# Second attention of a four-stage layer kernel: scores computed twice, once for the row maxima and once already transposed, with the position bias added by TensorE

## The chip, the cores and the metric

One core of one Trainium2 chip runs the whole program in one launch. The metric is device time in microseconds (us), the median of several executions. Smaller is better. One execution, taken by the hardware profiler, gives the rows shown here.

## The reference, cut to what matters

The input is 16 sequences of 512 tokens of width 128. Four layers follow each other, each with a residual and a layer norm: a first attention (cumulative sums), a first mixture of 8 experts, a second attention (softmax with a position bias), a second mixture of 8 experts. The change is in the second attention, and it borrows time in the first expert layer.

```python
table = jax.vmap(_fir_fft, in_axes=(0, None))(coeffs, proto).T
rel = jnp.abs(r[None, :] - r[:, None]).astype(jnp.float32) / max(S - 1, 1)
idx = jnp.clip(jnp.round(rel * (RES - 1)).astype(jnp.int32), 0, RES - 1)
pos_bias = jnp.einsum('ijf,hf->hij', table[idx], Wpos)
q, k, v = jnp.split(jnp.einsum('bsd,ed->bse', x, Wqkv), 3, axis=-1)      # 16 heads of 8 columns
logits = jnp.einsum('bihd,bjhd->bhij', q, k) * scale + pos_bias[None]
attn = jax.nn.softmax(logits, axis=-1)
out = jnp.einsum('bhij,bjhd->bihd', attn, v).reshape(B, S, D)
return jnp.einsum('bsd,ed->bse', out, Wout)
```

The bias of a head depends on the distance of query and key alone, so one line of numbers per head holds it all.

## The kernel before

The program is a chain of five stages with a barrier between each two: `attention_one`, `experts` with tag b, `attention_two` (tiles named c_), `experts` with tag d, `finish`. Each engine has a program of its own, and they meet through semaphores; the order on every engine is written out by hand.

`attention_two` (L1081) goes over 16 sequences, one `body` each. A body is 64 units: 16 heads times 4 blocks of 128 queries, each unit being 128 queries by 512 keys. For one unit:

- TensorE (PE) computes the scores (`scores`, L1351). Queries and keys are split into three bf16 parts and stacked, so the contraction has 72 rows and one bf16 matmul of 512 columns does it. It reads from the stacks `qst` and `kst`, which exist twice, one pair for each of two sequences.
- VectorE (DVE) adds the bias tile from SBUF and takes the row minimum of the negated scores (`biased`, L1613). Its result is a 128x512 tile `sums` and a column `low`.
- ScalarE (ACT) takes the exponential in place (`exps`, L1501).
- PE turns the tile with four f32 transposes (`turn`, L1360).
- ACT copies six of eight turned tiles to SBUF, DVE the other two, units 4 and 5 of each eight (`copy`, L1203; `DVE_TILES`, L1113).
- PE multiplies with the values (`values`, L1373). This is done in 32-column tiles of the array, four heads side by side, once for every second unit. A column of ones in the values gives the softmax's denominator.

PE runs six units ahead with scores and DVE five ahead with the bias; four PSUM banks hold scores. Between the units stand the small jobs of a sequence, called `others` on each engine (L1433, L1542, L1671): the front of the next sequence (`front_turn`, `front_qk`, `front_v`: sum of the expert result, layer norm, projection to q, k, v), the turning and division of a group of four heads (`out_turn`, `out_norm`), the tail of the last sequence (`tail_turn`, `tail_out`, layer norm) and its routing to the experts (`route_turn`, `route_logits`, `route_count`). A small job on PE waits in line for what ACT or DVE must deliver.

SyncE's queue carries, per sequence: `clear_rows` (2 MB of zeros, L171), the parts to DRAM (L1238), six transfers that build the stacks (`stack`, L1249), the load of `x1` (L1231) and the store of `x3` (L1254). GpSimd (POOL) does the power of -1/2 (`power`, L1299), the split in bf16 parts (`split`, L1174 and L1177), the gather and the scatter of rows.

The loop over sequences (`bodies`, L1210) has the first and the last body written out and seven passes of a hardware loop over two bodies each.

`experts` (L842) with tag b goes over 24 blocks of 512 tokens. Its SyncE queue loads `x` and `w` for each block (L921, L922), four buffers deep, and GpSimd has nothing to do there after one memset (L935).

## Time and profile before

| | us |
|---|---|
| median of 3 runs | 2395.94 |
| lowest, highest | 2393.09, 2398.47 |
| the profiled execution | 2393.4 |
| its span, first to last instruction | 2391.6 |

Busy time over the span: PE 2020.0 us (84%), weight loads 1300.1 us (54%, beside PE), DVE 1641.1 us (69%), ACT 1533.0 us (64%), POOL 797.4 us (33%). The granted TensorE clock is 0.939 of full speed over the span.

A share of the whole span mixes five stages with different limits. The second attention is a little over half of the span, so it has to be read by itself, in a window of its own. In the rows below a group is named by line, engine, operation and tiles; "out<-in" are the program's names.

### The profile page before, as it was taken

The page shows a single profiled execution, that of the slowest core. Times are in us where ns is not written, and L with a number is a line of the kernel's source. Part 1 is how long each engine was busy: PE and PEld are TensorE (multiplying, and loading weights), DVE is VectorE, ACT ScalarE, POOL GpSimd, SP SyncE. Part 2 cuts the span into 40 slices and gives each one's busy share as a digit, 9 for nine tenths or more (in the row PEclk, how much of TensorE's full clock was granted, in tenths as well). Part 3 has the DMA queues.
Part 4 walks back from the last instruction along what each step waited for, and adds up shares of the span by engine and source line. Part 5 has one row for each costly group of instructions (what it writes and reads, how often), then busy time and mean ns, then how long its engine had stood idle before and what let it go on. Part 6 is the DMA issues. An engine that isn't in the chain of part 4 may idle for free. (4 is left out here: it accounts for less than half of the span.)

```text
span 2391.6 us, 49680 instructions
## 1 busy us (share of the span) xinstructions
PE 2020.0 (84%) x14348; PEld 1300.1 (54%) x14348; DVE 1641.1 (69%) x4785; ACT 1533.0 (64%) x3427; POOL 797.4 (33%) x804
## 2 busy tenths in 40 slices
PE   8478887887494799999999999999999999779886
PEld 6256555566372455555555555555555555446553
DVE  6377888887212678877877788787778787633276
ACT  3355655564141688888888888888888888523221
POOL 4467888887101211222122122212211220000176
PEclk9788999999696899999999999999999999889998
DMA  3451332321263303320332033213311330034332
GB/s 112 149 211 67 106 105 103 103 101 62 96 214 126 112 31 97 107 87 34 97 107 81 28 107 107 57 53 108 102 44 70 107 93 11 10 130 164 112 103 83
DMA packets 114183, 227.10 MB, mean 95 GB/s; under 512 B 11684, under 2 KB 39332, under 8 KB 111604
## 3 DMA queue, kind: packets, MB, share of 16 engines
q1 hardware_dynamic: 105748, 207.36, 26.3%
q0 software_dynamic: 8192, 16.79, 2.2%
q8 instruction: 116, 1.90, 0.3%
q14 instruction: 127, 1.04, 0.1%
HBM read 177.86 MB, written 121.23 MB: 125 GB/s over the span
## 5 line engine op out<-in xcount | busy, mean ns | idle before, releaser
L1613 DVE CUSTOM_DVE_ANT_0 c_sums<-c_s,bias 128x512 f32<-128x512 f32 x1024 | 673.6, 687 | 180.2 <-PE c_s L1351 140.7
L1501 ACT ACTIVATE c_sums<-c_sums,c_low 128x512 f32<-128x512 f32 x1024 | 735.3, 743 | 39.1 <-DVE c_low L1613 28.2
L1360 PE MATMUL c_turned<-ident,c_sums 128*128 128x128 f32 x4096 | 633.4, 277 | 29.8 <-ACT c_pT L1203 27.8
L1360 PEld LDWEIGHTS c_turned<-ident,c_sums 128*128 128x128 f32 x4096 | 497.4, 142 | 181.2 <-ACT c_pT L1203 91.0
L1203 ACT COPY c_pT<-c_turned 128x512 f32<-128x512 f32 x768 | 454.7, 592 | 129.2 <-PE c_turned L1360 128.5
L1351 PE MATMUL c_s<-c_kst,c_qst 72*128 72x512 bf16 x1024 | 399.0, 391 | 45.9 <-DMA c_qst<-parts_d 27.5
L1373 PE MATMUL c_o<-c_pT,c_vst 128*32 128x256 f32 x4096 | 328.2, 393 | 0.7 <-ACT c_pT L1203 0.7
L1299 POOL TENSOR_TENSOR c_rstd<-c_ve,minus_half 128x4 f32<-128x4 f32 x32 | 32.9, 1027 | 638.1 <-DVE c_ve L122 638.1
L1203 DVE COPY c_pT<-c_turned 128x512 f32<-128x512 f32 x256 | 176.6, 690 | 86.0 <-PE c_turned L1360 83.9
L1351 PEld LDWEIGHTS c_s<-c_kst,c_qst 72*128 72x128 bf16 x1024 | 102.3, 100 | 232.3 <-issue 123.8
L520 ACT ACTIVATE v<-a_bank,gain 128x64 f32<-128x64 f32 x768 | 165.7, 344 | 53.9 <-DVE vp L734 53.9
L386 PE MATMUL a_bank<-wv,xT 128*128 128x512 f32 x256 | 153.4, 685 | 19.6 <-ACT v L520 15.1
L528 ACT COPY oT<-a_bank 128x512 f32<-128x512 f32 x128 | 69.5, 586 | 148.5 <-PE a_bank L407 148.5
L587 POOL TENSOR_TENSOR q<-q,vp 128x1024 f32<-128x1024 f32 x48 | 124.9, 2602 | 104.4 <-DVE vp L734 104.0
L598 POOL TENSOR_TENSOR s<-q,v 128x1024 f32<-128x1024 f32 x48 | 142.9, 2978 | 0.1
L1306 POOL DMA_INDIRECT zs_d<-c_xs,c_slot x64 | 62.7, 980 | 218.6 <-DVE c_slot L1669 202.0
L734 DVE TENSOR_TENSOR vp<-a_bank,ez 128x512 f32<-128x512 f32 x96 | 64.8, 687 | 102.4 <-PE a_bank L386 100.4
L415 PEld LDWEIGHTS a_bank<-wo,oT 128*128 128x128 f32 x1024 | 127.3, 200 | 14.3 <-issue 14.3
L415 PE MATMUL a_bank<-wo,oT 128*128 128x128 f32 x1024 | 129.6, 282 | 0.0
L1373 PEld LDWEIGHTS c_o<-c_pT,c_vst 128*32 128x32 f32 x4096 | 81.4, 108 | 87.3 <-issue 85.8
L407 PE MATMUL a_bank<-ident,o 128*128 128x128 f32 x512 | 80.4, 308 | 51.6 <-DVE o L750 50.8
L750 DVE TENSOR_TENSOR o<-o,r 128x1024 f32<-128x1024 f32 x64 | 123.6, 1951 | 0.0
(248 smaller groups left out, 2795.4 us busy)
## 6 DMA issues: line engine op xcount, KB each, us to landing
xs_d<-in_zeros SPq DMA_DIRECT2D x16, 2048.0 KB
zs_d<-in_zeros SPq DMA_DIRECT2D x16, 2048.0 KB, 24.8
c_kst<-parts_d SPq DMA_DIRECT2D x48, 384.0 KB
c_qst<-parts_d SPq DMA_DIRECT2D x48, 384.0 KB
parts_d<-c_parts SPq DMA_DIRECT2D x32, 384.0 KB, 2.5
d_w<-in_wd SPq DMA_DIRECT2D x24, 384.0 KB, 3.2
b_w<-in_wb SPq DMA_DIRECT2D x24, 321.0 KB, 3.1
bias_d<-line_d SPq DMA_DIRECT2D x16, 448.0 KB
```

Source lines behind the costliest of these rows:

```text
L386: nc.tensor.matmul(v_ps[h][:], xT[s.par][:, t, :], wv[:, 512 * h:512 * h + 512], start=True, stop=True).then_inc(sem("v_ready"), 1)
L415: mm = nc.tensor.matmul(y_ps[:, t * W:(t + 1) * W], oT[t % 2][:, k, :], wo[:, k, :], start=(k == 0), stop=(k == HA // P - 1))
L520: ins = nc.scalar.activation(dst[:, h * A:(h + 1) * A], v_ps[half][:, k * A:(k + 1) * A], ACT.Copy, scale=gain[s.par][:, t, h:h + 1])
L587: nc.gpsimd.tensor_tensor(q[:, t, :], q[:, t - 1, :], vp[t % 2][:], ALU.add).then_inc(sem("q_ready"), 1)
L598: nc.gpsimd.tensor_tensor(s1[s.par][:, t, :], q[:, t - 1, :], v2[t % 2][:], ALU.add).then_inc(sem("s1_ready"), 1)
L750: v.tensor_tensor(heads(o[t % 2][:]), heads(o[t % 2][:]), r[s.par][:, t, :].unsqueeze(2).to_broadcast([P, H, A]), ALU.mult).then_inc(sem(" ...
L1203: engine(pT[r % 2][:, :, m // 2, m % 2 * P:(m % 2 + 1) * P], pT_ps[m % 2][:]).then_inc(sem(copied(s, n)[0]), 1)
L1351: nc.tensor.matmul(s_ps[n % BANKS][:], qst[s.par][:, h, t * P:(t + 1) * P], kst[s.par][:, h, :], start=True, stop=True).then_inc(sem("s_ps ...
L1360: mm = nc.tensor.transpose(pT_ps[n % 2][:, c, :], sums[n % BUFS][:, c * P:(c + 1) * P], keep.ident[:])
L1373: mm = nc.tensor.matmul(o_ps[ARRAY * i:ARRAY * (i + 1), r % 2 * 2 * P:(r % 2 + 1) * 2 * P], vst[s.par][:, c, f:f + ARRAY], pT[r % 2][:, c, ...
L1501: nc.scalar.activation(sums[b][:], sums[b][:], ACT.Exp, bias=low[b][:], scale=-1.0).then_inc(sem("exp_done"), 1)
L1613: v.tensor_tensor_reduce(sums[n % BUFS][:], s_ps[n % BANKS][:], bias, 1.0, 3.0e38, ALU.add, ALU.min, low[n % BUFS][:]).then_inc(sem("low_r ...
```

## The change

The second attention is computed in two passes over the scores.

- **Pass one** (`scores`, `tops`): as before, but in group order, with DVE taking the row maximum and throwing the sum away. It runs 16 slots, half a sequence, ahead of pass two. A slot is two units.
- **The maxima** of a group of four heads (16 columns) are turned by PE (`tops_turn`), written as two bf16 parts (`tops_high` on ACT, `tops_low` on DVE), sent to DRAM and from there into rows 126 and 127 of `qst` (SyncE's `tops`). The same rows of `kst` hold -1. Rows 72 to 125 are zeros.
- **Pass two** (`below`, `biased`): a matmul over all 128 rows gives the scores transposed and less the maximum. Four bf16 matmuls in 32-column tiles add the bias from a tile `line`, in which each of 96 partitions holds the bias line shifted by one element, in three bf16 parts. ACT takes the exponential from PSUM straight into the layout that `values` needs. The four f32 transposes and the copies of ACT and DVE are gone, and so is the sum tile in SBUF as an input of ACT.
- `values` runs once per slot, right behind `biased`.
- One pair of stacks instead of two; the stacks are built in four parts, one for each group of four heads.
- The small jobs are divided over more slots, and the front is made two sequences ahead instead of one.
- `line` is prepared on GpSimd in `experts` b: three bf16 parts to DRAM, then 16 transfers that spread it, each let go by one finished block.
- At the start DVE clears partitions 64 to 127 of both stacks with two memsets of 8192 bf16 elements per partition. Three bodies are written out before the loop and three behind it; the loop has five passes of two.

```diff
+        def spread_line(pool):
+            pool.wait_ge(sem("line_out"), 16)
+            LAST = LINE - ARRAY
+            flat = keep.line[:].rearrange("r h d n -> r (h d n)")
+            PIECES = 4
+            for k in range(PIECES):
+                first, past = LINE // PIECES * k, min(LINE // PIECES * (k + 1), LAST)
+                for a in range(LINE_PARTS + 1):
+                    pool.wait_ge(sem("y_ps"), PIECES * k + a + 1)
+                    src = bass.AP(io["lparts_d"].tensor, a % LINE_PARTS * LINE + first, [[1, ARRAY], [1, past - first]])
+                    pool.dma_start(flat[ARRAY * a:ARRAY * (a + 1), first:past], src).then_inc(sem("line_in"), 16)
...
-    LEAD = 6
-    DVE_LEAD = 5
-    ACT_LEAD = 2
-    BANKS = 4
-    BUFS = 8
-    DVE_TILES = (4, 5)
+    SLOTS = ALL // 2
+    PER = TILES // 2
+    LEAD = 2 * PER
+    BANKS = 3
...
         def bodies(eng, body, own=None, per=0):
-            body(at(0), tail=False)
-            with eng.Fori(0, NB // 2 - 1) as i:
+            for k in range(3):
+                body(at(k), Flags(k > 0, True, True))
+            with eng.Fori(0, (NB - 6) // 2) as i:
...
+                def stack(s, j):
+                    for w in range(2):
+                        sp.wait_ge(sem(f"parts_out{w}"), 16 * s.b + 16)
+                        apart(sp, sem("sp_passed"))
+                    need(sp, sem("u_ps"), ALL * (s.b - 1) + TILES * (j + 1))
...
+                def tops(s, j):
+                    sp.wait_ge(sem("m_ready"), group_of(s, j) + 1)
+                    sp.dma_start(io["tops_d"].rearrange("a i p -> i a p"), mT[:]).then_inc(sem("m_out"), 16)
+                    sp.wait_ge(sem("m_out"), 16 * group_of(s, j) + 16)
+                    apart(sp, sem("sp_passed"))
+                    sp.dma_start(qst[ROWS_MAX:P, G * j:G * j + G, :].rearrange("r h n -> r (h n)"),
+                                 io["tops_d"].rearrange("a i p -> a (i p)")).then_inc(sem(f"m_in{j}"), 16)
...
+                def body(s, on):
+                    if not isinstance(s.b, int) or s.b > 0:
+                        stack(s, 3)
+                    if on.front:
+                        load(s.ahead().ahead())
+                    tops(s, 1)
+                    if on.nxt:
+                        put_parts(s.ahead())
+                        stack(s.ahead(), 0)
+                    tops(s, 2)
+                    if on.tail:
+                        store(s.back())
+                    if on.nxt:
+                        stack(s.ahead(), 1)
+                    tops(s, 3)
                     clear_rows(sp, "zs_d", s.b, io, sem("rows_clear"))
+                    if on.nxt:
+                        stack(s.ahead(), 2)
+                        tops(s.ahead(), 0)
...
+                def below(s, n):
+                    j, c, i = unit(n)
+                    if n % TILES == 0:
+                        pe.wait_ge(sem(f"m_in{j}"), 16 * s.b + 16)
+                    need(pe, sem("exp_done"), freed(s, n))
+                    h = G * j + i
+                    nc.tensor.matmul(u_ps[bank_of(n)][:], kst[:, h, c * P:(c + 1) * P], qst[:, h, :],
+                                     start=True, stop=False, skip_group_check=True)
+                def biased(s, n):
+                    j, c, i = unit(n)
+                    for k in range(P // ARRAY):
+                        u = P - ARRAY - ARRAY * k
+                        mm = nc.tensor.matmul(u_ps[bank_of(n)][ARRAY * k:ARRAY * (k + 1), :].rearrange("k (t q) -> k t q", t=T), pick[:],
+                                              line[:, G * j + i, T - 1 - c:DELTA - c, u:u + P], start=False, stop=True,
+                                              skip_group_check=True)
+                    mm.then_inc(sem("u_ps"), 1)
...
+                def body(s, on):
+                    for p in range(SLOTS):
+                        u = 2 * (p + LEAD)
+                        if u < ALL:
+                            scores(s, u)
+                            scores(s, u + 1)
+                        elif on.nxt:
+                            scores(s.ahead(), u - ALL)
+                            scores(s.ahead(), u - ALL + 1)
+                        below(s, 2 * p)
+                        below(s, 2 * p + 1)
+                        biased(s, 2 * p)
+                        biased(s, 2 * p + 1)
+                        if p >= 2:
+                            values(s, (p - 2) // 2, p % 2)
+                        elif on.tail:
+                            values(s.back(), SETS - 1, p)
+                        others(s, p, on)
...
                 def exps(s, n):
-                    act.wait_ge(sem("low_ready"), ALL * s.b + n + 1)
-                    b = n % BUFS
-                    nc.scalar.activation(sums[b][:], sums[b][:], ACT.Exp, bias=low[b][:], scale=-1.0).then_inc(sem("exp_done"), 1)
+                    act.wait_ge(sem("u_ps"), ALL * s.b + n + 1)
+                    if n % G == 0:
+                        need(act, sem("pv_done"), SETS * s.b + n // G - 1)
+                    nc.scalar.activation(pT[n // G % 2][:, n % G, :], u_ps[bank_of(n)][:], ACT.Exp).then_inc(sem("exp_done"), 1)
...
+                def body(s, on):
+                    for p in range(SLOTS):
+                        exps(s, 2 * p)
+                        others(s, p, on)
+                        exps(s, 2 * p + 1)
+                        if p % PER == 1 and (p > 1 or on.tail):
+                            out_copy(*((s, p // PER - 1) if p > 1 else (s.back(), GROUPS - 1)))
...
                 v = nc.vector
                 own = Own(dve, sem("own"), sem("dve_passed"))
+                v.memset(minus[:], -1.0).then_inc(sem("minus_ready"), 1)
+                v.memset(kst[64:P], 0.0).then_inc(sem("pad_ready"), 1)
+                v.memset(qst[64:P], 0.0).then_inc(sem("pad_ready"), 1)
```

On PE the small jobs stand at the end of a slot: `tail_out` in slot 9, `route_logits` in slot 17, `front_qk` in slots 30 and 31, each a slot or two behind the turn that feeds it. ACT's copy for them stands between the two exponentials of slots 9, 17, 30 and 31.

## Rows read from the trace of the kernel before

**Rows 1.** Page, section 2: 40 slices of the span, PE's busy tenths and its clock

```profile
PE   8478887887494799999999999999999999779886
PEclk9788999999696899999999999999999999889998
```

**Rows 2.** Stretches: length; busy PE, PEld, DVE, ACT, POOL; clock; DMA share; GB/s

```profile
739.00:789.50 50.50, 7.28 (x16) 3.53 (x17) 8.69 (x24) 2.55 (x7) 10.50 (x13) 0.50 0.40 127
789.50:2072.70 1283.20, 1203.73 (x10128) 729.20 (x10128) 1017.89 (x3346) 1099.82 (x2006) 251.48 (x280) 0.99 0.24 75
650.00:700.00 50.00, 49.85 (x305) 36.98 (x305) 8.30 (x12) 23.73 (x39) 0.00 (x0) 1.00 0.66 215
```

**Rows 3.** PE in order of time in the regular part: start us, length us

```profile
1267.69 0.64 PE L1373 MATMUL c_o<-c_pT,c_vst 128*32 128x256 f32 x8
1268.26 0.39 PE L1351 MATMUL c_s<-c_kst,c_qst 72*128 72x512 bf16 x1
1268.49 0.60 PE L1360 MATMUL c_turned<-ident,c_sums 128*128 128x128 f32 x4
1268.93 0.38 PE L1351 MATMUL c_s<-c_kst,c_qst 72*128 72x512 bf16 x1
...
1271.96 0.66 PE L1360 MATMUL c_turned<-ident,c_sums 128*128 128x128 f32 x4 [0.22 <-ACT c_pT L1203]
```

**Rows 4.** The last products with the values, PE in order of time

```profile
2070.07 1.94 PE L1373 MATMUL c_o<-c_pT,c_vst 128*32 128x256 f32 x32 [0.73 <-ACT c_pT L1203]
```

**Rows 5.** Small jobs on PE in one sequence, in order of time

```profile
1286.92 1.13 PE L1394 MATMUL c_misc<-c_xT,c_wq 128*128 128x512 f32 x2
1287.88 0.38 PE L1351 MATMUL c_s<-c_kst,c_qst 72*128 72x512 bf16 x1
...
1295.79 0.66 PE L1406 MATMUL c_misc<-ident,c_att 128*128 128x128 f32 x4
1296.28 0.38 PE L1351 MATMUL c_s<-c_kst,c_qst 72*128 72x512 bf16 x1
```

**Rows 6.** Groups by line: busy us, mean ns of one

```profile
L1862 ACT ACTIVATE e_gate<-e_bank 128x512 f32<-128x512 f32 x32 | 19.1, 597 | 84.7 <-PE e_bank L1821 84.7
L1631 DVE COPY c_x<-c_x 128x512 f32<-128x512 f32 x16 | 6.8, 423 | 0.0
```

**Rows 7.** DVE in order of time: two bias additions that follow each other

```profile
790.90 0.69 DVE L1613 CUSTOM_DVE_ANT_0 c_sums<-c_s,bias 128x512 f32<-128x512 f32 x1
791.51 0.69 DVE L1613 CUSTOM_DVE_ANT_0 c_sums<-c_s,bias 128x512 f32<-128x512 f32 x1
```

**Rows 8.** A back edge of the loop: a stretch, and PE's first row after it

```profile
1350.00:1354.00 4.00, 2.85 (x13) 2.16 (x14) 2.64 (x7) 2.46 (x5) 0.00 (x0) 0.74 0.04 8
1351.15 0.39 PE L1351 MATMUL c_s<-c_kst,c_qst 72*128 72x512 bf16 x1 [2.70 <-issue]
```

**Rows 9.** Start of the second attention, all engines in order of time

```profile
745.05 1.28 POOL L1326 MEMSET c_vst<- 128x668 f32 x2
746.75 0.69 DVE L1593 TENSOR_TENSOR c_yb<-c_yb,prob 128x512 f32<-128x512 f32 x1 [7.45 <-DMA c_yb<-ys_d,c_rows]
...
766.28 2.30 SPq L1249 DMA_DIRECT2D c_qst<-parts_d  x3
...
789.50 3.37 PE L1351 MATMUL c_s<-c_kst,c_qst 72*128 72x512 bf16 x7 [27.52 <-DMA c_qst<-parts_d]
```

**Rows 10.** Page, section 6: transfers, KB each, median us to landing

```profile
zs_d<-in_zeros SPq DMA_DIRECT2D x16, 2048.0 KB, 24.8
...
parts_d<-c_parts SPq DMA_DIRECT2D x32, 384.0 KB, 2.5
...
b_x<-xs_d SPq DMA_DIRECT2D x24, 256.0 KB, 2.6
...
c_x<-x_d SPq DMA_DIRECT2D x16, 256.0 KB, 22.6
```

More of the change, by code:

```diff
@@ L1198, in copy, with unit @@
[L1198 to L1208 removed]
+        def unit(n):
+            j, n = n // TILES, n % TILES
+            return j, n // G, n % G
@@ L1556, in others @@
+                    if on.tail and p == 21:
                         route_exp(s.back())
-                def body(s, tail=True, front=True):
-                    for j in range(GROUPS):
-                        for n in range(SLOTS):
-                            k = SLOTS * j + n
-                            if later(s, k + ACT_LEAD, front):
-                                exps(*later(s, k + ACT_LEAD))
-                            if n % ROUND_SLOTS not in DVE_TILES:
-                                copy(s, k, act, nc.scalar.copy)
-                            others(s, j, n, tail, front)
+                    if on.nxt and p == 27:
+                        tops_high(s.ahead(), 0)
@@ L1605, in biased, with stats @@
[L1605 to L1614 removed]
+                def stats(src, st, some):
+                    for t in some:
+                        own.did(v.bn_stats(st[:, t, :], src[:, t, :]))
@@ new lines, in spread, with scaled @@
+                def spread(st, mv, ve, ready):
+                    own.wait(alone=True)
+                    for t in range(T):
+                        own.did(v.bn_aggr(mv[:, t, :], st[:, t, :]))
+                    own.wait()
+                    v.tensor_scalar(ve[:], mv[:, :, 1], EPS, None, ALU.add).then_inc(ready, 1)
+                def scaled(src, dst, mv, rstd, some):
+                    for t in some:
+                        ins = v.tensor_scalar(dst[:, t, :], src[:, t, :], mv[:, t, 0:1], rstd[:, t:t + 1], ALU.subtract, ALU.mult)
+                    return ins
@@ L1694, in body @@
-                def body(s, tail=True, front=True):
-                    for j in range(GROUPS):
-                        for n in range(SLOTS):
-                            k = SLOTS * j + n
-                            if later(s, k + DVE_LEAD, front):
-                                biased(*later(s, k + DVE_LEAD))
-                            if n % ROUND_SLOTS in DVE_TILES:
-                                copy(s, k, dve, v.tensor_copy)
-                            others(s, j, n, tail, front)
@@ L1704, in _, with early @@
-                front_sum(at(0))
-                front_stats(at(0))
-                front_apply(at(0), 1)
-                split(at(0), dve, v, own)
-                for n in range(DVE_LEAD):
-                    biased(at(0), n)
+                def early(s, p, on):
+                    if on.tail and p == 10:
+                        tail_sum(s.back())
+                    if on.tail and p == 18:
+                        route_tops(s.back())
+                    if p == 29:
+                        out_norm(s, 2)
@@ L1934, in program @@
         stage(attention_one)
+        keep.line = sb("spread_line", [P, H, DELTA, UPAD], BF16)
         if stages >= 2:
```

600 lines of the change are left out of this document (387 added, 213 removed).

## Prediction, before the result was known

> **What bounds the kernel now.** First the page's 40 slices, to see the stages: PE is at nine tenths from slice 15 to 34 with the clock near full, and that stretch is the second attention [rows 1]. Then the busy time by stretch, to leave the other stages out: the loop of the second attention lasts 1283.2 us, 80.2 for each of 16 sequences; PE is busy for 1203.7 of them, ACT for 1099.8, DVE for 1017.9 [rows 2]. So PE is the fullest engine, and the change is worth what it takes out of PE's line, its pauses included. That is read in PE's own order of time, from start to start, since matmuls overlap. A score matmul holds PE 0.22 to 0.23 us, four transposes 0.44, a step of `values` 0.57 (1267.69 to 1268.26) [rows 3].
>
> **PE per slot of two units, before.** Two scores 0.44, two turns 0.88, one step of `values`. The last 32 instructions of `values`, with nothing between, take 1.94 us for four steps, less some 0.2 for the end of the last: 0.43 a step [rows 4]. Against 0.57 that leaves 0.14 for going back from 32-column tiles to the whole array [rows 3]. Going in costs about 0.10 (estimate: a turn holds PE 0.53 when `values` follows it, 0.44 when not). Sum 0.44 + 0.88 + 0.43 + 0.24 = 1.99.
>
> **PE per slot, after.** Two scores 0.44. Two `below`, bf16 of 512 columns like a score, 0.44. Eight matmuls of `biased`, in two sets of four side by side: no row shows bf16 in such tiles. The nearest is `values`: 8 f32 matmuls of 256 columns in 0.43, so four of them side by side take 0.213; f32 runs at half the rate per column (two of 512 columns hold PE 0.96 [rows 5], one bf16 0.22), so a set of bf16 with 512 columns moves the same bytes and should also take 0.213. The bounds are that, and no overlap at all, 4 x 0.213 = 0.85. I take 0.215 a set, 0.43 for both, since the f32 row has the full overlap and the same bytes. `values` 0.43, one way in and out 0.24, as before. Sum 1.98. **The two forms cost PE the same**: a transpose set of 0.44 is exchanged for 0.22 + 0.215. What the change can win is only PE's pauses.
>
> **The floor of a sequence.** 32 slots x 1.98 = 63.4. Small jobs: seven turns of four transposes at 0.49 = 3.4 (1295.79 to 1296.28 is one of them); the projection of q 0.96 (1286.92 to 1287.88) [rows 5]; k, v, output and logits stream as much or less, I take 0.9 each, and 0.5 for the counts: 4.1. That is 8.5. New are four `tops_turn`, one transpose each, some 0.15 = 0.6 (a quarter of 0.44 and a little). Sum 9.1, floor 63.4 + 9.1 = 72.5 against 80.2 now, so 7.7 us per sequence are pauses today: PE waits for a copy of ACT or DVE from the two turned banks (0.22 at 1271.96 [rows 3]), and at each of six back edges of the loop nothing comes for 2.70 us and the clock is at 0.74 of full for the next four [rows 8], together some 4.7.
>
> **What takes their place.** The chain sum, exponential, turn, copy is gone. ACT has 64 exponentials straight from PSUM; the nearest row without a bias operand is a Silu of that shape, 597 ns [rows 6], so 38 us and some 7 of copies in 72. DVE has 64 x 0.61 = 39 us of maxima [rows 7] and about 16.6 us of small work, as now: 56 of 72, with work of at most 2.6 us in the fullest slots against 2.0 and three PSUM banks to even it out. Neither is a bound. But four small jobs get a new wait. Output, logits and both projections on PE stand at the end of a slot (1.98), and ACT's copy for them stands behind the first exponential of the same slot. That starts when `biased` of the first unit is done, 0.88 + 0.10 + 0.215 and 0.17 of latency, at 1.4; the exponential holds ACT 0.5, the copy 0.6: ready at 2.5, **0.6 us late, four times: 2.4 us per sequence**. Behind the waiting matmul all of PE stands, scores of the next slot included. ACT and DVE then wait for those. I add 1 us per sequence for other coincidences. Four back edges instead of six: 4 x 4.7 = 19.
>
> **Sum of the loop.** 16 x 72.5 = 1160. The first sequence has no tail (-3.7), the last two no front (-5.7), and the last 16 slots have no scores (-7): 1143.5. Waits 2.4 x 15 and 1 x 16: 52. Back edges 19. Together 1214.5, and 1.7 for the last products.
>
> **The start.** Now the first score starts at 789.50, since the stacks, issued until 768.6, land only then, and the first gathered rows reach DVE at 746.75 [rows 9]. After: two memsets on DVE stand ahead of that. No DVE memset is in the trace. POOL clears 2 x 668 elements in 1.28, which gives 7.8 us for 8192 and 15.7 for both; DVE's fastest copy, 512 elements in 423 ns [rows 6], gives 6.8 each by length. I take 15.7: from 739.3 to 755, so 8.5 late (if they run twice as fast, 7.5 us of idle time hides nearly all). The Trainium skill ("VectorE: DVE Perf Modes", section "Zero memsets can be issued as uint32 (trn2)") says that a memset takes one cycle per element whatever the type, and half of that for bf16 zeros issued as uint32; that would be either end of the same bounds. The first quarter of the stacks should land 6 us after its issue instead of 21 to 24, so scores start at about 784. Then 32 units come before the first `below`, at DVE's pace: 0.61 x 32 = 20 us, to 804, and the maxima's way through DRAM ends about then. The loop ends at 804 + 1216 = 2020, against 2072 now: -52.
>
> **Experts b.** The 16 transfers of `line` are some 0.46 MB each, about one per block of 3.9 us, beside 215 GB/s and a DMA share of 0.66 while PE is full [rows 2]: 118 GB/s more, and 215 / 0.66 = 326 in all is just what there is. A block's input lands in 2.6 us today [rows 10] and is due after one block; later landing stops PE. Bounds 0 and 25 us; I take 6. The split on GpSimd is hidden by the plan of the blocks. The rest is unchanged. **Total -46**: 2393.4 - 46 = 2347 in the profiled execution, whose time is 2.5 under the median: 2350.
>
> **Rivals.** **A, slower: the maxima come late.** Each group's maxima must be in `qst` four to five slots after DVE has them, 9 to 11 us; two transfers that follow each other cost 5 (2.5 each, as the parts [rows 10]). They stand in SyncE's line behind a quarter of the stacks and behind 2 MB of zeros. Before, 256 KB of `x1` behind the stacks took 22.6 us and the zeros 24.8 [rows 10]: small transfers do wait for big ones. A quarter is 6 us, the zeros alone some 6 (2 MB at the 326 GB/s above); I find 5 us of slack for the next sequence's first group. If quarters take twice as long, it is used up; 5 us beyond that cost 15 x 5 = 75: 2350 + 75 = 2425. For: the 22.6. Against: zeros are issued some 14 us earlier. **B, slower: four bf16 streams don't fit side by side.** A quarter more per set, 0.054 x 1024 = 55: 2405; no overlap of pairs, 0.215 x 1024 = 220: 2570. For: no row of bf16. Against: the f32 row. The Trainium skill ("TensorE: Matmul & The Clock Gate", section "Measured speedup vs the span model") measured a speedup of 2.38 for three column tiles, not 3, about the first of these prices; the trace's four f32 streams come close to 4. **C, faster: the waits vanish**, since ACT runs further ahead than I think, memsets and experts cost nothing: 52 + 8.5 + 6 less, 2285. **D: nothing comes of it**: DVE's lumps stop the scores for 3 us per sequence: 2350 + 46 = 2396.
>
> **How the numbers follow.** My forecast (2315 to 2385) 0.50; A 0.19; B 0.08; C 0.13; D 0.10. 0.2% is 4.8 us, what a measurement of this kernel can tell from none. D is spread over both sides of it, as are the weak forms of A. Faster 0.70, same 0.05, slower 0.25. The range leaves out the better half of C and B's and A's upper parts: 2300 to 2440.
>
> **What would show it.** Right: PE's order of time in a slot has 0.22, 0.22, 0.22, 0.22, then 16 instructions of 32-column tiles in about 0.9, slots of 2.0 without a small job, 2.6 plus the job in slots 9, 17, 30 and 31 with PE waiting for ACT's copy, and about 76 us per sequence. DVE busy for three quarters, ACT for under two thirds. Wrong: PE waiting for a transfer into `qst` (A), more than 0.25 us per set of `biased` (B), scores waiting for DVE (D), PE's experts b blocks longer than 3.9 us by over 1.

## The result, and the profile after the change

The changed kernel takes **2328.02 us** (median of 4 runs, 2325.22 to 2330.99), beside 2396.62 us for the kernel before (4 runs, 2393.09 to 2398.47): a ratio of 0.972, 95% interval 0.970 to 0.973, or 68.6 us less. Forecast were 2350 us and a range of 2300 to 2440. The profiled execution has a span of 2325.9 us, 65.7 less than before.

The page of the changed kernel: busy times, the 40 slices, and the costliest groups with busy us, mean ns of one, and the idle time ahead of them.

```profile
PE 1985.4 (85%) x15436; PEld 1034.3 (44%) x15436; DVE 1502.4 (65%) x4596; ACT 1078.8 (46%) x2723; POOL 807.6 (35%) x827
PE   8488787877388499999999999999999999679886
PEclk9689999999699699999999999999999999889998
L1622 ACT ACTIVATE c_pT<-c_u 128x512 f32<-128x512 f32 x1024 | 574.6, 596 | 552.1 <-PE c_u L1429 552.1
L1777 DVE CUSTOM_DVE_ANT_0 c_sums<-c_s,bias 128x512 f32<-128x512 f32 x1024 | 665.1, 687 | 254.2 <-PE c_s L1411 229.5
```

PE is again at nine tenths, from slice 15 to 34 as before [rows 1], but of a shorter span. ACT fell from 1533.0 us to 1078.8, DVE from 1641.1 to 1502.4, and both stand idle mostly because PE has not delivered. So PE sets the pace as before. By stage, in the two profiled executions; an expert stage begins with its first GpSimd memset, the second attention with DVE's first instruction (739.1 and 765.7 us):

| stage | before | after | difference | forecast |
|---|---|---|---|---|
| up to experts b | 626.6 | 628.8 | +2.2 | 0 |
| experts b | 112.5 | 136.9 | +24.4 | +6 |
| second attention | 1361.6 | 1272.5 | -89.1 | -52 |
| experts d and finish | 290.9 | 287.7 | -3.2 | 0 |
| span | 2391.6 | 2325.9 | -65.7 | -46 |

The sum is 20 us off, out of two errors of opposite sign: experts b lost 18 more, and the second attention won 37 more. That the sum is nearer than its terms is luck.

**The regular part**, PE in order of time (start, length), one slot from `scores` to `scores`:

```profile
1223.70 0.60 PE L1411 MATMUL c_s<-c_kst,c_qst 126*128 126x512 bf16 x2
1224.14 0.60 PE L1421 MATMUL c_u<-c_qst,c_kst 128*128 128x512 bf16 x2
1224.66 0.61 PE L1429 MATMUL c_u<-spread_line,c_pick 128*32 128x512 bf16 x8
1225.11 0.60 PE L1443 MATMUL c_o<-c_pT,c_vst 128*32 128x256 f32 x8
1225.64 0.60 PE L1411 MATMUL c_s<-c_kst,c_qst 126*128 126x512 bf16 x2
```

Starts lie 0.44, 0.52, 0.45 and 0.53 us apart: 1.94 us a slot, with nothing waited for. The way into the 32-column tiles is the 0.08 over 0.44 behind `below`, the way out the 0.10 over 0.43 behind `values`.

**PE's waits** from 900 to 1900 us (us in all, times, longest), the whole list of the changed kernel:

```profile
PE c_s L1411 <- issue: 11.5, 4, 3.0
PE c_misc L1469 <- ACT c_xT L1638: 7.7, 13, 0.6
PE c_misc L1486 <- ACT c_xT L1657: 7.4, 14, 0.5
PE c_misc L1469 <- ACT c_qk L1643: 7.3, 13, 0.6
PE c_misc L1498 <- ACT c_xT L1661: 6.9, 13, 0.5
PE c_s L1411 <- DVE c_tops L1777: 2.3, 10, 0.2
```

Four times per sequence 0.5 to 0.6 us for a copy of ACT, four back edges of up to 3.0 us, and next to nothing else. No line names a transfer, and none does from 765 to 2030 us: the maxima were never late. The same turn of a small job, one sequence apart, gives the period, 74.26 us:

```profile
1211.30 0.66 PE L1480 MATMUL c_misc<-ident,c_att 128*128 128x128 f32 x4
...
1214.33 1.16 PE L1486 MATMUL c_misc<-c_wout,c_xT 128*128 128x128 f32 x8 [0.53 <-ACT c_xT L1657]
...
1285.56 0.66 PE L1480 MATMUL c_misc<-ident,c_att 128*128 128x128 f32 x4
```

Before, the same turn came after 78.86 us (1216.93 to 1295.79 [rows 5]). These are sequences without a back edge of the loop. The four with one last 78.63 to 79.02 us, so a back edge costs 4.4 to 4.8.

**The start**, DVE and PE in order of time:

```profile
766.83 3.47 DVE L1721 MEMSET c_kst<- 64x4096 uint32 x1 [0.91 <-issue]
771.11 3.47 DVE L1722 MEMSET c_qst<- 64x4096 uint32 x1 [0.80 <-issue]
...
802.48 2.59 PE L1411 MATMUL c_s<-c_kst,c_qst 126*128 126x512 bf16 x5
...
822.98 1.06 PE L1421 MATMUL c_u<-c_qst,c_kst 128*128 128x512 bf16 x2
```

The first score comes 36.8 us after the stage's first instruction (50.4 before [rows 9]), the first `below` 57.3 after it.

**Experts b.** First the ten microseconds from 650 of the changed kernel (length; busy PE, PEld, DVE, ACT, POOL; clock; DMA share; GB/s), then what PE waited for there between 650 and 765:

```profile
650.00:660.00 10.00, 9.14 (x58) 6.54 (x57) 1.38 (x2) 4.37 (x7) 0.99 (x2) 1.00 1.01 268
...
PE b_bank L1093 <- DMA b_x<-xs_d: 15.2, 10, 3.7
```

Before, the stage ran at a share of 0.66 and 215 GB/s with PE never idle [rows 2]. Now the share is at its top while only 268 GB/s move, and PE waits ten times for the input of a block. The waits are not the whole cost. One of them, in order of time, and the stretch 666 to 667 us behind it:

```profile
663.91 0.66 PE L1093 MATMUL b_bank<-ident,b_x 128*128 128x128 f32 x4 [2.37 <-DMA b_x<-xs_d]
...
669.57 0.60 PE L1093 MATMUL b_bank<-ident,b_x 128*128 128x128 f32 x4
...
666.00:667.00 1.00, 1.00 (x7) 1.00 (x6) 0.00 (x0) 0.69 (x1) 0.00 (x0) 0.50 0.98 330
```

Behind each of the three longest waits (2.37, 3.12 and 3.69 us) the granted clock is 0.50, its lower level of 1.2 GHz, and that block takes 5.7 to 6.6 us instead of 3.94. Of the 24.4 us, 15.5 are waits (16.5 us behind the stage's first input against 1.0 before), some 6 are the clock (estimate: busy time times the missing clock, over slices of 1 us), and 1.0 is a later first block; the last 2 are not traced.

### The profile page after: what moved, and what is told of

It is laid out like the page before. It is cut to its first block and busy times, and to the rows that moved or that the text cites. A ratio compares the mean times of both kernels' runs of the same rounds, so it can differ in the third digit from the quotient of the medians.

```text
span 2325.9 us, 49229 instructions
## 1 busy us (share of the span) xinstructions
PE 1985.4 (85%) x15436; PEld 1034.3 (44%) x15436; DVE 1502.4 (65%) x4596; ACT 1078.8 (46%) x2723; POOL 807.6 (35%) x827
## 5 line engine op out<-in xcount | busy, mean ns | idle before, releaser
L1622 ACT ACTIVATE c_pT<-c_u 128x512 f32<-128x512 f32 x1024 | 574.6, 596 | 552.1 <-PE c_u L1429 552.1
L1411 PE MATMUL c_s<-c_kst,c_qst 126*128 126x512 bf16 x1024 | 319.0, 389 | 16.9 <-issue 11.5
L1429 PE MATMUL c_u<-spread_line,c_pick 128*32 128x512 bf16 x4096 | 317.2, 387 | 0.0
L1443 PE MATMUL c_o<-c_pT,c_vst 128*32 128x256 f32 x4096 | 310.9, 381 | 0.6 <-ACT c_pT L1622 0.5
L1421 PE MATMUL c_u<-c_qst,c_kst 128*128 128x512 bf16 x1024 | 307.7, 381 | 0.2 <-ACT c_pT L1622 0.2
L1443 PEld LDWEIGHTS c_o<-c_pT,c_vst 128*32 128x32 f32 x4096 | 123.1, 110 | 107.4 <-ACT c_pT L1622 4.0
L1429 PEld LDWEIGHTS c_u<-spread_line,c_pick 128*32 128x32 bf16 x4096 | 61.8, 94 | 217.7 <-issue 217.7
L1421 PEld LDWEIGHTS c_u<-c_qst,c_kst 128*128 128x128 bf16 x1024 | 100.2, 98 | 121.1 <-issue 5.8
L1411 PEld LDWEIGHTS c_s<-c_kst,c_qst 126*128 126x128 bf16 x1024 | 82.7, 100 | 158.9 <-DVE c_tops L1777 101.9
L737 DVE TENSOR_TENSOR vp<-a_bank,ez 128x512 f32<-128x512 f32 x96 | 64.8, 687 | 106.8 <-PE a_bank L389 105.0
L418 PEld LDWEIGHTS a_bank<-wo,oT 128*128 128x128 f32 x1024 | 126.7, 199 | 14.4 <-issue 14.4
L1356 POOL TENSOR_TENSOR c_rstd<-c_ve,minus_half 128x4 f32<-128x4 f32 x16 | 16.7, 1046 | 298.4 <-DVE c_ve L1746 298.4
```

The source lines that it names most:

```text
L418: mm = nc.tensor.matmul(y_ps[:, t * W:(t + 1) * W], oT[t % 2][:, k, :], wo[:, k, :], start=(k == 0), stop=(k == HA // P - 1))
L1411: nc.tensor.matmul(s_ps[bank_of(n)][:], qst[0:ROWS_MAX, h, t * P:(t + 1) * P], kst[0:ROWS_MAX, h, :], start=True, stop=True).then_inc(sem( ...
L1421: nc.tensor.matmul(u_ps[bank_of(n)][:], kst[:, h, c * P:(c + 1) * P], qst[:, h, :], start=True, stop=False, skip_group_check=True)
L1429: mm = nc.tensor.matmul(u_ps[bank_of(n)][ARRAY * k:ARRAY * (k + 1), :].rearrange("k (t q) -> k t q", t=T), pick[:], line[:, G * j + i, T - ...
L1443: mm = nc.tensor.matmul(o_ps[ARRAY * i:ARRAY * (i + 1), half * 2 * P:(half + 1) * 2 * P], vst[s.par][:, c, f:f + ARRAY], pT[r % 2][:, i, h ...
L1622: nc.scalar.activation(pT[n // G % 2][:, n % G, :], u_ps[bank_of(n)][:], ACT.Exp).then_inc(sem("exp_done"), 1)
```

## The experiments

The twelve kernels ran in three groups on three chips. The kernel before took 2400.5 us beside the first group, 2496.1 beside the second and 2488.0 beside the third, so times are compared inside a group or as ratios to the kernel before. Only the third group has the changed kernel itself; the first is set beside the result, where the kernel before took 2396.6, and the 2331 of the 72 rows bears that out. Stage lengths are read between the same two instructions in each trace: "experts b" from its first GpSimd memset to DVE's memset of `kst` (138.0 in the changed kernel), "second attention" from there to the first GpSimd memset of experts d (1271.4). Among the kernels that leave the transfers as they are, experts b ranges from 132.4 to 138.0, so a few us there mean nothing.

| kernel | chip | us | ratio to before | experts b | second attention |
|---|---|---|---|---|---|
| no transfers | 1 | 2301.79 (1 run) | | 114.3 | 1272.3 |
| copy first | 1 | 2284.69 | 0.952 (0.949-0.954) | 136.1 | 1230.4 |
| one stream | 1 | 2330.41 (1 run) | | 133.5 | 1270.4 |
| 72 rows | 1 | 2331.18 | 0.971 (0.969-0.973) | 136.0 | 1273.4 |
| two edges | 2 | 2370.23 | 0.950 (0.947-0.953) | 133.3 | 1294.9 |
| 24 transfers | 2 | 2370.30 | 0.948 (0.945-0.951) | 126.2 | 1308.3 |
| bias twice | 2 | 2579.46 (1 run) | | 132.4 | 1509.5 |
| three together | 2 | 2320.84 | 0.929 (0.927-0.932) | 131.5 | 1250.8 |
| changed kernel | 3 | 2369.34 | 0.953 (0.950-0.956) | 136.5 | 1311.0 |
| split clearing | 3 | 2360.95 | 0.949 (0.946-0.951) | 120.0 | 1317.1 |
| three, split | 3 | 2301.76 | 0.926 (0.924-0.928) | 122.1 | 1254.9 |
| two edges again | 3 | 2363.11 | 0.950 (0.948-0.952) | 133.9 | 1296.6 |

**Are the transfers the cause of the longer experts b?** All 16 transfers of `spread_line` are left out and one GpSimd memset clears the line, so the output lacks the bias.

```diff
-            for k in range(PIECES):
-                first, past = LINE // PIECES * k, min(LINE // PIECES * (k + 1), LAST)
-                for a in range(LINE_PARTS + 1):
...
-                    pool.dma_start(flat[ARRAY * a:ARRAY * (a + 1), first:past], src).then_inc(sem("line_in"), 16)
...
+            nc.gpsimd.memset(keep.line[:], 0.0).then_inc(sem("line_in"), 16)
...
```

> Left out: the 16 transfers that spread the bias line in experts b; GpSimd clears the tile instead, so the output is computed without the bias. Theory (the transfers and the blocks' own loads share the 16 DMA engines, and loads that land late stop PE): experts b falls back from 136.9 us to about 113 us, blocks every 3.94 us from first to last, the landing of b_x back from 3.9 to 2.6 us, the total 2328 - 23 = 2305. Rival (GpSimd's split of the line, its semaphore waits or the plan cost the time, not the transfers): experts b stays above 125 us, since the split is still there. The second attention does not change under either.

Experts b shrinks from 138.0 to 114.3 us while the second attention stays (1272.3), and the time is 2301.8. The same ten microseconds as above in this kernel:

```profile
650.00:660.00 10.00, 10.00 (x64) 7.50 (x63) 1.38 (x2) 5.42 (x9) 4.66 (x1) 1.00 0.55 176
```

Share 0.55 and PE full. The split of the line is still there, so the transfers are what lengthens the stage: 24 us.

**Are the four waits worth what they seem?** ACT's copies of the slots where PE waits stand ahead of the slot's first exponential.

```diff
                     for p in range(SLOTS):
+                        if p in (9, 17, 30, 31):
+                            others(s, p, on)
                         exps(s, 2 * p)
-                        others(s, p, on)
+                        if p not in (9, 17, 30, 31):
+                            others(s, p, on)
                         exps(s, 2 * p + 1)
```

> ACT's copy for the small jobs stands ahead of the first exponential in slots 9, 17, 30 and 31, instead of behind it; nothing else is changed. Theory (PE is the only bound of the loop and loses 0.53 to 0.61 us four times per sequence to this order): the four waits of PE go to about 0, a sequence goes from 74.3 to 72.1 us, the total falls by 2.2 x 15 = 33 us to 2295 (2290 to 2302). Rival 1 (the exponential that is now late by 0.5 us stops PE instead, at below of the next slot or at values): total within 10 us of 2328, with new waits of PE for ACT's exponential. Rival 2 (DVE's maxima are as near to the bound as PE): gain under 15 us, with PE waiting for DVE's maxima.

2284.69 us, 43 under the result and 5 below the range expected; the second attention is 41.0 us shorter. All of PE's waits that are left between 900 and 1900 us, and the same place as above, in order of time:

```profile
PE c_s L1411 <- issue: 8.8, 4, 2.3
PE c_s L1411 <- DVE c_tops L1780: 2.3, 10, 0.2
...
1197.82 0.66 PE L1480 MATMUL c_misc<-ident,c_att 128*128 128x128 f32 x4
...
1200.25 1.16 PE L1486 MATMUL c_misc<-c_wout,c_xT 128*128 128x128 f32 x8
1201.25 0.60 PE L1411 MATMUL c_s<-c_kst,c_qst 126*128 126x512 bf16 x2
...
1202.21 0.62 PE L1429 MATMUL c_u<-spread_line,c_pick 128*32 128x512 bf16 x8
```

The projection follows its turn after 2.43 us instead of 3.03. Nothing is given back: `biased` follows `scores` after 0.96 us in both kernels (1201.25 to 1202.21 here), so the exponential that is late by one copy stops nothing. The period falls from 74.26 to 71.77 us (1197.82 to 1269.59), 15 x 2.49 = 37 us, and the four back edges cost 2.7 less: 40 of the 41.

**Do four bf16 streams lie side by side?** Three of the four matmuls of each `biased` are left out, so the bias reaches a quarter of the rows only.

```diff
-                    for k in range(P // ARRAY):
+                    for k in range(1):
                         u = P - ARRAY - ARRAY * k
```

> Left out: three of the four column tiles of the bias matmuls (12 of 16 are gone per pair of units), so the bias is missing for three quarters of the keys. Theory (four bf16 streams of 512 columns run side by side in the time of one): PE's step from the start of the bias matmuls to values stays at 0.44 us for two units, the slot at 1.94, the total within 6 us of 2328. Rival (the streams share a port and are only partly side by side, one set costing more than one stream): the step falls below 0.44 towards its share; were they serial in pairs, it would be 0.22 per stream now and the time would fall by 0.2 per slot, some 100 us. A single stream of 512 bf16 columns for each of two units can't take less than 0.43 in all if it is the same tile.

2330.41 us, and the second attention lasts 1270.4 us against 1271.4. The slot in this kernel, PE in order of time:

```profile
1223.30 0.60 PE L1411 MATMUL c_s<-c_kst,c_qst 126*128 126x512 bf16 x2
1223.74 0.60 PE L1421 MATMUL c_u<-c_qst,c_kst 128*128 128x512 bf16 x2
1224.27 0.39 PE L1429 MATMUL c_u<-spread_line,c_pick 128*32 128x512 bf16 x1
1224.28 0.42 PE L1443 MATMUL c_o<-c_pT,c_vst 128*32 128x256 f32 x3
1224.50 0.38 PE L1429 MATMUL c_u<-spread_line,c_pick 128*32 128x512 bf16 x1
1224.52 0.78 PE L1443 MATMUL c_o<-c_pT,c_vst 128*32 128x256 f32 x5
1225.24 0.60 PE L1411 MATMUL c_s<-c_kst,c_qst 126*128 126x512 bf16 x2
```

One stream takes 0.23 us to the next, four took 0.22: the slot is 1.94 in both. `values` now starts 0.01 us behind the first bias matmul, in the tiles that it leaves free; but the slot is no shorter, since one tile still has both bias matmuls and its part of `values` to do. What that tile does is the price of a set, and the other three streams are free.

**What does a set cost, and is PE really the bound?** Each unit gets a second set of four with a weight tile of zeros.

```diff
+                    for k in range(P // ARRAY):
+                        u = P - ARRAY - ARRAY * k
+                        nc.tensor.matmul(u_ps[bank_of(n)][ARRAY * k:ARRAY * (k + 1), :].rearrange("k (t q) -> k t q", t=T), nil[:],
+                                         line[:, G * j + i, T - 1 - c:DELTA - c, u:u + P], start=False, stop=False,
+                                         skip_group_check=True)
...
```

> Each unit gets four more bf16 matmuls in 32-column tiles, with a weight tile of zeros, ahead of the four that add the bias; nothing is left out and the sums stay the same. Theory: in the second attention PE is what sets the pace, and a set of four side by side costs what the stack of four costs in the forecast, 0.215 us: 1024 sets x 0.215 = 220 us more, 2328 + 220 = 2548. If a set only needs the time of one stream without the way in and out, and the way out of the tiles was 0.10 of it, 1024 x 0.11 = 113: 2441. Rival: ACT or DVE sets the pace in most slots; then the first part of the added time vanishes in their slack and the kernel stays under 2400.

2579.46 us, 209 more than the two other kernels on that chip that keep the order of ACT (2370). PE in order of time:

```profile
1223.27 0.61 PE L1413 MATMUL c_s<-c_kst,c_qst 126*128 126x512 bf16 x2
1223.72 0.60 PE L1423 MATMUL c_u<-c_qst,c_kst 128*128 128x512 bf16 x2
1224.24 0.40 PE L1431 MATMUL c_u<-spread_line,c_nil 128*32 128x512 bf16 x4
1224.47 0.39 PE L1436 MATMUL c_u<-spread_line,c_pick 128*32 128x512 bf16 x4
1224.68 0.39 PE L1431 MATMUL c_u<-spread_line,c_nil 128*32 128x512 bf16 x4
1224.90 0.39 PE L1436 MATMUL c_u<-spread_line,c_pick 128*32 128x512 bf16 x4
1225.12 0.60 PE L1450 MATMUL c_o<-c_pT,c_vst 128*32 128x256 f32 x8
```

A set takes 0.21 to 0.23 us. 1024 x 0.22 = 225; the stage grew by 201 (1509.5 against 1308.3). The rest are waits of PE that the longer slot swallows: those for ACT's four copies fell from 35 us to 24, those for ACT's exponentials from 16.4 to 3.0 and those for DVE's maxima from 15.9 to 1.6, while 13 us came up of which the profile names no releaser. Nine tenths of what is added to PE's line is paid: it is the bound.

**Do the filled rows cost anything?** The scores of pass one read 72 rows instead of 126.

```diff
-                    nc.tensor.matmul(s_ps[bank_of(n)][:], qst[0:ROWS_MAX, h, t * P:(t + 1) * P], kst[0:ROWS_MAX, h, :],
+                    nc.tensor.matmul(s_ps[bank_of(n)][:], qst[0:ROWS_QK, h, t * P:(t + 1) * P], kst[0:ROWS_QK, h, :],
```

> The scores of pass one contract over the 72 rows that hold data instead of 126 (the pad rows are zeros), as before the change; nothing else is changed. Theory (the filled rows cost nothing and bring nothing while PE is kept busy by other work): total within 5 us of 2328, granted clock as before at 0.98 to 1.00 in the loop. Rival (the clock follows how much of the array is in use, so the filled rows keep it up): the clock falls in parts of the loop, and the time rises by 10 us or more.

2331.18 us, ratio 0.971 as the changed kernel; its second attention lasts 1273.4, and the granted clock from 900 to 1900 us is 0.99 in both. The filled rows neither cost nor bring time that can be told from noise.

**Two back edges instead of four.** Five bodies are written out on each side of the loop. The first run had no changed kernel on its chip beside it, so it was run again.

```diff
-            for k in range(3):
+            for k in range(5):
                 body(at(k), Flags(k > 0, True, True))
-            with eng.Fori(0, (NB - 6) // 2) as i:
+            with eng.Fori(0, (NB - 10) // 2) as i:
...
+            body(at(NB - 5), Flags(True, True, True))
+            body(at(NB - 4), Flags(True, True, True))
...
```

> Five sequences are written out ahead of the hardware loop and five behind it, so the loop has three passes and two back edges instead of four; nothing else is changed. Theory: each back edge costs PE 2.7 to 3.0 us in which nothing comes and about 2 us at a lower clock behind it, 4.7 in all, so two fewer give 9.4 us: 2328 - 9 = 2319, ratio to the kernel before 0.968 against 0.972 of the changed kernel, and PE's waits at c_s for nothing that the profile shows fall from 4 times to 2. Rival: the written-out sequences cost as much in another place (more instructions to fetch once each), then 2324 to 2332 and the same ratio as the changed kernel.

> Two back edges instead of four and nothing else, now beside the changed kernel on the same chip. Theory: 9.4 us under it (2 x 4.7), 0.4 percent. Rival: the sequences written out cost as much elsewhere, no difference over 3 us. In the one profile at hand PE's waits at the back edge are 2 instead of 4, 6.3 us instead of 11.9, so that the direct part should be 5.6 us at least.

The first run gave a ratio of 0.950, far below the expected 0.968, which is the chip's doing. On the third chip 2363.11 against 2369.34: 6.2 us, with intervals of the ratios that overlap, so that the time alone does not tell 9.4 from 3. PE's wait at the back edges from 790 to 2030 us, the changed kernel of that chip first:

```profile
PE c_s L1411 <- issue: 12.0, 4, 3.4
```

```profile
PE c_s L1413 <- issue: 6.3, 4, 3.2
```

The direct part of 5.7 us is there. The stage is 14.3 us shorter in these profiles, and 13.4 between the two kernels of the second chip; 3.0 of the 14.3 are waits behind the pauses told of below (7.8 less for ACT's exponentials, 4.8 more for DVE's maxima), and the slower clock behind an edge is in the rest. From turn to turn, as above, the four edges of the changed kernel cost 2.6 to 4.8 us each on this chip, 16.0 together, and the two here 8.3. That is 7.8 for two. But a sequence written out also lasts 75.8 to 76.3 us there and one in the loop 77.5 to 77.7, where the result's trace has 73.9 and 74.3; with four more written out, that is as much again, and why is open. The forecast 9.4 lies between what the times and the traces say, and that two edges alone bring it is not shown.

**What of the transfers costs the time?** They become 24 of half the size, one for each block; the last 32 partitions are cleared by GpSimd. First in one memset ahead of them:

```diff
-            PIECES = 4
+            PIECES = 8
+            nc.gpsimd.memset(keep.line[ARRAY * LINE_PARTS:P], 0.0).then_inc(sem("line_clear"), 1)
...
-                for a in range(LINE_PARTS + 1):
-                    pool.wait_ge(sem("y_ps"), PIECES * k + a + 1)
+                for a in range(LINE_PARTS):
+                    need(pool, sem("y_ps"), LINE_PARTS * k + a)
...
```

> The bias line is spread in 24 transfers of half the size, one for each block of experts b, and its last 32 partitions are cleared by GpSimd in place of four transfers. 5.4 MB are moved instead of 7.2 MB, evenly over the stage. Theory: the 24 us that experts b became longer come from the bandwidth that the 16 large transfers take in single blocks (DMA share 1.0, loads of x late by more than the buffers give); with the load spread, about 120 GB/s less at the peak, the stage lasts 113 to 120 us instead of 137: 2328 - 17 to - 24 = 2304 to 2311, ratio 0.962 to 0.965. Rival: the sum of bytes sets it (then 24 x 5.4 / 7.2 = 18 us remain of the 24): 2322, ratio 0.969. Second rival: the layout of the source rows, each starting one element further, costs by the number of rows and not by their size: then 24 transfers of 32 rows against 16 of 32 are no cheaper, 2328 or more.

The stage still lasted 126.2 us, 7 less than the 133.3 of its neighbour on the chip, and the time, 2370.30, is the neighbour's; the expected 0.962 to 0.965 can't be judged there, without the changed kernel. The experiment had a fault of its own, seen in the GpSimd rows of the kernel with all three edits:

```profile
654.28 23.99 POOL L930 MEMSET spread_line<- 32x28672 bf16 x1 [2.02 <-DMA lparts_d<-b_lparts]
678.22 2.47 POOL L936 DMA_DIRECT2D spread_line<-lparts_d  x5
...
693.14 1.11 PE L1095 MATMUL b_bank<-ident,b_x 128*128 128x128 f32 x4 [7.79 <-DMA b_x<-xs_d]
```

The memset holds GpSimd for 24 us, and five transfers then leave at once, with a sixth in the same 3 us. PE, which had not waited since the second block, stands still for 7.79 us. So the clearing was split into eight memsets, each ahead of three transfers:

```diff
             for k in range(PIECES):
                 first, past = LINE // PIECES * k, min(LINE // PIECES * (k + 1), LAST)
+                nc.gpsimd.memset(flat[ARRAY * LINE_PARTS:P, first:past], 0.0).then_inc(sem("line_clear"), 1)
```

> The changed kernel itself, as the measure for the three others, since the edits of two edges and of 24 transfers ran on a chip where the kernel before took 2496 us instead of 2397 and no run of the changed kernel stands beside them. Expected: if that chip comes again, the two of these runs that share the loop and the waits with it (two edges 2370, 24 transfers 2370) put it at 2375 to 2385, ratio 0.952 to 0.955; on a chip like the first, 2328 to 2333, ratio 0.971.

2369.34 us, ratio 0.953, as expected for a chip of this kind.

> The bias line is again spread in 24 half-size transfers, one for each block of experts b, but the last 32 partitions are cleared by GpSimd in eight memsets of 3 us, one ahead of every third transfer, instead of one of 24 us that held back the first transfers and let four of them go together. Theory: the 24 us of experts b come from transfers that meet in the same block; spread evenly, with 5.4 MB instead of 7.2, the stage falls from 137 us to 113 to 122: 15 to 24 us under the changed kernel of the same job, 0.6 to 1.0 percent. Rival: bytes alone decide, three quarters of them cost 18 us: 6 us under it. Second rival: the number of rows decides, 24 x 32 against 16 x 32: no gain or up to 10 us slower.

Experts b 120.0 us against 136.5 of the changed kernel on that chip: 16.5 less, inside the forecast of this theory, while three quarters of the bytes would have left 18 of 24. The time fell by only 8.4 us, with intervals of the ratios that overlap: in the profiled execution experts b began 8.3 us later (638.9 against 630.6) and the second attention lasted 6.2 longer, neither of which the edit touches. First the 80 us from 660 in the changed kernel on that chip, then in this one:

```profile
660.00:740.00 80.00, 64.77 (x360) 45.22 (x359) 10.38 (x15) 28.67 (x45) 6.40 (x13) 0.96 0.90 243
```

```profile
660.00:740.00 80.00, 76.32 (x453) 54.04 (x452) 13.14 (x19) 35.46 (x56) 28.62 (x26) 1.00 0.88 252
```

Mean share and bandwidth are nearly the same, and PE is busy for 76.3 us instead of 64.8. That is not an equal load: the line now takes half as much per block, 0.23 MB instead of 0.46, and PE gets through more blocks. Two causes are at work, and they are only in part taken apart. The mean load is one: beside the blocks' 215 GB/s the line wanted 118, 333 in all, where 268 to 275 move at a share of one. That stretches 16 blocks of 3.94 us by 13 to 15 us (estimate), about what PE waited; with half the line per block, 274 are wanted and almost nothing is left. Lumps are the other: the two kernels with the single memset move the same bytes as the two with the split one, and have experts b of 126.2 and 131.5 us against 120.0 and 122.1.

**The three together.**

> Three edits together: ACT makes the copy of a small job ahead of the first exponential of the slot where PE waits for it (slots 9, 17, 30 and 31), the loop has two back edges instead of four, and the bias line is spread in 24 even transfers. Theory: they lie in different places, so they add up: 44 us of the first (2328 - 2285, as measured alone), 9 of the second, 17 to 24 of the third: 2251 to 2258, ratio to the kernel before 0.939 to 0.943. Rival: without the waits another limit is near (DVE at 65 percent of the span, ACT's line), and part of it is taken back: 2265 to 2280.

2320.84 us, 49.5 less than its two neighbours on the second chip, each of which has one of the three edits. The ratio 0.929 is below the expected 0.939 to 0.943, but it can't be compared with one from another chip.

> ACT's copy of four small jobs first, two back edges, and the 24 transfers with the split clearing, together. Theory: 44 + 9 + 15 to 24 us under the changed kernel of the same job, ratio to it 0.967 to 0.971, and 0.939 to 0.943 to the kernel before on a chip like the first. Rival: once the waits are gone, pauses of DVE and ACT reach PE, as on the chip where the three together took 2321: then 50 us or less under the changed kernel, ratio to it 0.979 or more.

With the split clearing 2301.76 us, 67.6 less than the changed kernel beside it (ratio 0.9715): experts b 14.4, second attention 56.1. The edits add up, to the lower end of the 68 to 77 that were expected, and the rival of 50 or less did not come, and this version beats both kernels: 0.926 of the kernel before.

**Pauses of ACT and DVE on two of the chips.** The changed kernel itself is 41 us slower on the third chip than in the result, nearly all in the second attention (1311.0 against 1271.4). Its waits from 790 to 2030 us, then an ACT row:

```profile
PE c_u L1421 <- ACT c_pT L1622: 18.2, 15, 1.5
PE c_s L1411 <- DVE c_tops L1777: 17.0, 23, 1.6
...
1112.15 1.08 ACT L1622 ACTIVATE c_pT<-c_u 128x512 f32<-128x512 f32 x2 [3.36 <-remote]
```

ACT stands still for over 3 us, 15 times in 1000 us, and the profile names no instruction of the core as the cause; in the result's trace there is no such wait. ACT's and DVE's slack takes up most of each, and PE sees 1.6 us of one at most: 18.2 + 17.0, less the 5.1 that stand in the same lines in the result, is 30.1 of the 39.6. What the pauses are stays open. On these chips the kernel before lost more (2488 against 2397), so the change is worth 4.7% there and 2.8% in the result; the trace of the kernel before on such a chip was not taken, so why is open too.

## Why the prediction was right, and where its terms were off

The direction and the mechanism were right: PE is the bound, the two forms cost PE much the same, and what the change wins is pauses. A sequence without a back edge fell from 78.86 to 74.26 us. The total was nearer than its terms: with experts b as forecast, the result would have been 2310 us, 40 under the forecast, so part of the small miss is luck.

- **The slot, 1.98 forecast, 1.94 measured.** Scores and `below` 0.44 each and a set of 0.22 were right. The way in and out was taken as 0.24, and is 0.08 + 0.10. 512 slots x 0.04 = 20 us, the largest single part of the 30 us by which the loop was shorter (1186 us from the first `below` at 822.98 to the last `values` at 2009.1, against 1216). The term had been taken from single differences of start times, 0.57 for `values` [rows 3] and 0.53 for a turn ahead of it; it is small, but stands there 512 times.
- **The four waits**, forecast at 0.6 us in slots 9, 17, 30 and 31, were measured at 0.5 to 0.6 there and nowhere else; moving the copies took them away. The prediction's own sum, ready at 2.5 in a slot of 1.98, gives 0.5 and not 0.6. The period is 74.26 us against 75.9, of which 32 x 0.04 = 1.3 is the slot. The 1 us for other coincidences was needed: 62.1 for slots, 9.1 for small jobs and 2.2 for waits leave 0.9.
- **Back edges** 4.7 each: 4.4 to 4.8 were measured, of which 3.0 at most is waiting.
- **The start.** Memsets were taken at 7.8 us each, and take 3.47 for 8192 bf16 elements per partition, as 4096 words. The slower bound was chosen because only an f32 row was there. The other bound, that they run twice as fast and hide, held: DVE's front sum came 1.5 us late, at 9.1 us after the stage's first instruction. The Trainium skill ("VectorE: DVE Perf Modes", section "Zero memsets can be issued as uint32 (trn2)") says that zeros in bf16 can be issued as half as many uint32 words, and the row has that form; that it halves the time no run here shows, since none has the other form at this size. The first `below` came 7.6 us earlier than forecast, of which 7.0 are this term; the 20 us for the first 32 maxima were right (20.5).
- **Experts b, the step that failed.** 6 us were taken between bounds of 0 and 25; it was 24.4. The working added mean rates, 215 + 118 GB/s against 326, and found that it just fits. That 326 was 215 divided by a share of 0.66, as if a share of one were worth as many bytes for every kind of transfer. Measured, a share of 1.01 moved 268 GB/s, and PE waited up to 3.7 us for one block's input. The slower clock behind the longest waits, some 6 us, was in neither bound. Half as much of the line per block, spread over all 24, took 16.5 us of the loss away.
- **Rival A** (maxima late) did not occur: no wait names `qst`, and the transfer behind which they might stand, 2 MB of zeros, lands sooner than before (24.8 us [rows 10]), as the page of the changed kernel shows:

```profile
zs_d<-in_zeros SPq DMA_DIRECT2D x16, 2048.0 KB, 10.0
```

- **Rival B** (streams not side by side) is refuted by the kernel with one stream and priced by the one with two sets. The Trainium skill ("TensorE: Matmul & The Clock Gate", section "Measured speedup vs the span model") gives 2.38 for three column tiles; here four bf16 tiles of 512 columns cost what one costs, so the measurement decides against it for this shape.
- **Rival C** (the waits vanish) came true only by another edit: with the copies first the time is 2285. **Rival D** (DVE's lumps stop the scores) is 2.3 us in 1000 on this chip.

## What to carry to other kernels

When an engine is the bound, order its instructions by start time and price the slot to 0.01 us, switches of tile shape included, for that term stands hundreds of times; then look, for every small job on it, at what stands ahead of its feeder on the other engine, since four copies moved by one exponential were worth 41 us here. Work that is moved into another stage because it "has room" must be judged twice: by the bandwidth that is measured with both kinds of transfer under way, and by how long its pieces hold up one load that is due soon. A wait can cost more than its length, through the clock behind it. And an edit measured alone needs the unchanged kernel on the same chip beside it.

## What the runs showed of the hardware that had not been expected

- Four bf16 matmuls of 512 columns in 32-column tiles take 0.22 us, and one alone 0.23.
- DVE clears 64 partitions x 4096 words in 3.47 us, 0.85 ns a word; GpSimd needed 23.99 us for 28672 bf16 elements per partition, 0.84 ns for each element, so half of DVE's rate per byte and partition.
- With transfers of rows that start one element further each beside the loads of the stage, a DMA share of 1.01 moved 268 GB/s in ten microseconds, where the loads alone moved 215 at 0.66.
- Behind waits of 2.37 to 3.69 us in experts b the granted clock was 0.50, and a block took 5.7 to 6.6 us instead of 3.94.
- The same kernel took 2328 us on one chip and 2369 on another, with pauses of 3 us on ACT and DVE that the profile does not explain.
